# Attention of two layers with each pair of heads stacked in two halves of the partitions

## What is computed

```python
# layer 2, causal, written as an online softmax over key blocks of 128;
# layer 0 is the same without the mask and with biases on q, k, v
scores = scale * jnp.einsum('bhtd,bhsd->bhts', Q, kb)
scores = jnp.where(future[None, None], -jnp.inf, scores)
m_new = jnp.maximum(m, jnp.max(scores, axis=-1, keepdims=True))
p = jnp.exp(scores - m_new)
l = corr * l + jnp.sum(p, axis=-1, keepdims=True)
acc = corr * acc + jnp.einsum('bhts,bhsd->bhtd', p, vb)
return acc / jnp.maximum(l, 1e-12)
```

## Time and profile before

| | |
|---|---|
| median of three runs | 1496.15 us (1493.22 to 1500.85) |
| the profiled execution | 1497.72 us, span 1496.0 us |
| granted TensorE clock, mean | 0.846 |
| busy: PE, DVE, ACT, POOL | 1135.4, 952.6, 614.8, 486.2 us |
| of the chain that ended last: PE, DVE, DMA | 46%, 23%, 7% |

### The profile page before, as it was taken

The page is one execution under the profiler, slowest core; times in us unless marked ns, Lnnn a source line. Parts: engine busy times, 40 slices in busy tenths (PEclk is TensorE's granted clock), DMA queues, the critical chain, the costliest instruction groups (busy, mean ns, idle before and its releaser), DMA issues.

```text
span 1496.0 us, 32177 instructions
## 1 busy us (share of the span) xinstructions
PE 1135.4 (76%) x9171; PEld 822.8 (55%) x9171; DVE 952.6 (64%) x3478; ACT 614.8 (41%) x1352; POOL 486.2 (32%) x695
## 2 busy tenths in 40 slices
PE   2799899889199994776728998999976899337950
PEld 1355555554188883664516776777654566225730
DVE  3688888886423324996836776777557687761237
ACT  1266556656044441335403554555554232113410
POOL 6112433434535453233441111111024111352553
PEclk9599889989599996997657999999977797558985
DMA  4655445531367767211025443444010000133523
GB/s 118 72 59 62 70 67 76 69 59 40 115 196 201 207 198 228 74 43 32 18 31 70 53 53 48 52 55 47 17 29 28 22 25 11 44 110 92 167 78 91
DMA packets 152567, 117.02 MB, mean 78 GB/s; under 512 B 16001, under 2 KB 140674, under 8 KB 152322
## 3 DMA queue, kind: packets, MB, share of 16 engines
q1 hardware_dynamic: 145282, 101.18, 34.2%
q0 software_dynamic: 7168, 14.37, 2.9%
HBM read 47.26 MB, written 23.41 MB: 47 GB/s over the span
## 4 chain that ended last, share of the span: by engine, by line
PE 46%; DVE 23%; issue 10%; DMA 7%; POOL 6%; SPq 3%; ACT 3%; DVEq 1%; POOLq 0%; ACTq 0%
PE po L1485 7%; PE po L431 6%; DVE xg L334 4%; PE pt L1479 4%; DVE mx L601 4%; PE pm L1479 3%; SPq L367 3%; PE pt L391 2%; PE pt L394 2%; PE pm L412 2%; DMA xs<-xg 2%; POOL rstd L327 2%; PE pm L417 2%; PE pm L418 2%; PE p L522 2%
## 5 line engine op out<-in xcount | busy, mean ns | idle before, releaser
L601 DVE TENSOR_REDUCE mx<-pm 128x2 f32<-128x512 f32 (+1 forms) x512 | 306.3, 619 | 163.2 <-PE pm L418 97.8
L553 ACT ACTIVATE ex<-pt 128x512 f32<-128x512 f32 (+1 forms) x512 | 271.1, 544 | 207.9 <-PE pt L391 99.3
L324 POOL TENSOR_SCALAR ve<-mv 128x2 f32<-128x2 f32 x96 | 25.5, 266 | 560.6 <-DVE mv L318 560.6
L1562 POOL DMA_INDIRECT result<-ye,to_row x128 | 122.9, 960 | 151.3 <-issue 107.2
L431 PE MATMUL po<-ex,va 128*32 128x256 f32 (+1 forms) x2048 | 157.7, 381 | 5.2 <-ACT ob L562 5.2
L412 PE MATMUL pm<-ks,qs 96*128 96x256 bf16 x512 | 110.7, 303 | 11.5 <-DVE mx L601 10.9
L308 ACT COPY xt<-p 128x256 f32<-128x256 f32 x112 | 41.8, 373 | 175.1 <-PE p L304 175.1
L1485 PE MATMUL po<-he,we 128*128 128x256 f32 (+1 forms) x448 | 112.9, 395 | 0.6 <-DVE yt L1523 0.4
L334 DVE TENSOR_SCALAR xg<-res,mv,rstd 128x128 f32<-128x128 f32 (+1 forms) x192 | 90.1, 536 | 32.6 <-POOL rstd L327 32.6
L391 PE MATMUL pt<-qs,ks 99*128 99x256 bf16 x512 | 105.7, 292 | 6.4 <-DMA qs<-mt 3.1
L303 PE MATMUL p<-ident,xs 128*128 128x128 f32 x112 | 40.4, 361 | 85.2 <-DMA xs<-xg 81.9
(11 more groups left out here) (281 smaller groups left out, 2788.5 us busy)
## 6 DMA issues: line engine op xcount, KB each, us to landing
we<-in_pack SPq DMA_DIRECT2D x40, 514.5 KB
xs<-xg SPq DMA_DIRECT2D x112, 128.0 KB, 2.2
qs<-parts SPq DMA_DIRECT2D x192, 64.0 KB
ks<-parts SPq DMA_DIRECT2D x192, 64.0 KB
we<-in_pack SPq DMA_DIRECT2D x16, 512.0 KB
xe<-sorted SPq DMA_DIRECT2D x56, 132.0 KB, 2.2
yr<-result SPq DMA_DIRECT2D x48, 128.0 KB, 2.2
xr<-xg SPq DMA_DIRECT2D x32, 128.0 KB, 4.8
```

The source lines that it names most:

```text
L553: nc.scalar.activation(ex[j % 2][:, 2 * u:2 * u + 2, lo:S], pt[:, u, :].rearrange("p (b k) -> p b k", k=S)[:, :, lo:S], ACT.Exp).then_inc( ...
L601: nc.vector.tensor_reduce(mx[q.slot % 2][:, qt, 4 * b + 2 * u:4 * b + 2 * u + 2], pm[:, u, :].rearrange("p (b k) -> p b k", k=S)[:, :, 0:h ...
L1562: pool.indirect_dma_start(out=rows, out_offset=bass.IndirectOffsetOnAxis(ap=to_row[q.slot][0:m, i:i + 1], axis=0), in_=ye[q.slot][0:m, i, ...
```

## The change

A pair of heads shares a slot in `qs` and `ks`: the even head in partitions 0 to 63 (`HALF`), the odd one in 64 to 127. Each has 48 rows of parts and three for the maximum in its half. The tensors are half as wide (`HP` = 8 slots). `scores_t` and `scores_m` become one function, `scores`, that issues a product for the maxima from one half and one for the exponents from the other in turn, after all its waits; in u = 0 the maxima take the even heads and the exponents the odd ones, in u = 1 the other way round. The mask is added by two products a `u` and side, over two heads at once, 128 and 64 columns a head, each from the 64 rows of a half (`half_id`, `hide_k`, `hide_q`). q and k are projected so that even and odd heads land in different halves (`by_half`), the biases are brought into that order once at the start, the maxima are transposed in two pieces, and each stack DMA is now two, one for each half of `parts`. The memsets of the stacks on POOL are gone; DVE fills rows 32 to 63 of each half of `ks` with ones before the data. POOL builds the masks with twelve affine selects in place of two.

```diff
-        hide_k = sb("hide_k", [P, P], BF16)
-        hide_q = sb("hide_q", [P, P], BF16)
+        half_id = sb("half_id", [P, 2, P], BF16)
+        hide_k = sb("hide_k", [P, 2, P], BF16)
+        hide_q = sb("hide_q", [P, 2, P], BF16)
...
-        STACK, MAX_AT = 48, 96
-        ks = [sb(f"ks{i}", [MAX_AT + 3, HEADS, S], BF16) for i in range(SLOTS)]
+        STACK, HALF, HP = 48, P // 2, HEADS // 2
+        ks = [sb(f"ks{i}", [P, HP, S], BF16) for i in range(SLOTS)]
...
-            qs = [sb(f"qs{i}", [MAX_AT + 3, HEADS, S], BF16, mem) for i in range(SLOTS)]
+            qs = [sb(f"qs{i}", [P, HP, S], BF16, mem) for i in range(SLOTS)]
...
-            mx = [sb(f"mx{i}", [P, 2, HEADS], F32, mem) for i in range(2)]
-            mr = [sb(f"mr{i}", [P, 2, HEADS], F32, mem) for i in range(2)]
-            mp = [sb(f"mp{i}", [P, 2, 3, HEADS], BF16, mem) for i in range(2)]
-            mt = [sb(f"mt{i}", [96, P], BF16, mem) for i in range(2)]
+            mx = [sb(f"mx{i}", [P, 2, 2, HP], F32, mem) for i in range(2)]
+            mr = [sb(f"mr{i}", [P, 2, 2, HP], F32, mem) for i in range(2)]
+            mp = [sb(f"mp{i}", [P, 2, 2, 3, HP], BF16, mem) for i in range(2)]
+            mt = [sb(f"mt{i}", [STACK, S], BF16, mem) for i in range(2)]
...
                     sp.wait_ge(mt_sb, a + q.n + 1)
-                    for t in range(2):
-                        sp.dma_start(qs[q.slot][MAX_AT:MAX_AT + 3, :, t * P:t * P + P],
-                                     mt[q.slot % 2][STACK * t:STACK * t + STACK, :]).then_inc(mrows[q.slot], 16)
+                    for of_pair in range(2):
+                        r = HALF * of_pair + STACK
+                        sp.dma_start(qs[q.slot][r:r + 3, :, :],
+                                     mt[q.slot % 2][3 * HP * of_pair:3 * HP * (of_pair + 1), :]).then_inc(mrows[q.slot], 16)
                 if (q := at(1)):
                     wait_apart(sp, parts_pool, 2 * (a + q.n + 1), passed)
+                    if a == 0:
+                        sp.wait_ge(consts_v, CONSTS_V)
+
                     wait_apart(sp, ts_ps, 16 * (a + q.back(3)), passed)
-                    sp.wait_ge(stack_zero, SLOTS * (2 if a == 0 else 3))
-
                     for r, of in enumerate(PAIRS):
                         for i, stack in enumerate((qs, ks)):
-                            sp.dma_start(stack[q.slot][r * DH:r * DH + DH, :, :].rearrange("r h k -> r (h k)"),
-                                         parts[q.slot % 2][:, of[i], i, :]).then_inc(stacked[q.slot], 16)
+                            for of_pair in range(2):
+                                rows_of = slice(HALF * of_pair + r * DH, HALF * of_pair + r * DH + DH)
+                                sp.dma_start(stack[q.slot][rows_of, :, :].rearrange("r h k -> r (h k)"),
+                                             parts[q.slot % 2][HALF * of_pair:HALF * of_pair + HALF, of[i], i, :]
+                                             ).then_inc(stacked[q.slot], 16)
...
+        def by_half(dst, left, right):
+
+            for of_pair in range(2):
+                last = nc.tensor.matmul(dst[HALF * of_pair:HALF * of_pair + HALF], left[:, of_pair::2], right,
+                                        start=True, stop=True)
+            return last
...
-            def scores_t(q, j, u):
...
-            def scores_m(q, j, u):
...
+            def half(stack, q, g, k, at_head):
+
+                return stack[q.slot][HALF * g:HALF * g + k, at_head, :]
+
+            def scores(qt, jt, qm, jm, u):
+
+                gm, gt = u, 1 - u
+                mine, theirs = pm[:, u, :], pt[:, u, :]
+                bm, qtile = jm // 2, jm % 2
+                bt, ktile = jt // 2, jt % 2
+                if qt:
+                    pe.wait_ge(stacked[qt.slot], SPLITS * (a // SLOTS + qt.turn + 1))
+                    pe.wait_ge(mrows[qt.slot], 32 * (a // SLOTS + qt.turn + 1))
+                    wait(pe, e_sb, 16 * (a + qt.n) + 2 * jt + u - 1)
+                if qm:
+                    if jm == 0:
+                        pe.wait_ge(stacked[qm.slot], SPLITS * (a // SLOTS + qm.turn + 1))
+                    wait(pe, ms_max, 16 * (a + qm.n) + 2 * jm + u - 1)
+                if causal:
+                    at_q, at_k = qtile * P, ktile * P
+                    rows_m, rows_t = slice(HALF * gm, HALF * gm + HALF), slice(HALF * gt, HALF * gt + HALF)
+                    for first in (True, False):
+                        lo = 0 if first else HALF
+                        if qm:
+                            dst = mine.rearrange("p (e k) -> p e k", k=S)[:, :, at_q + lo:at_q + P]
+                            pe.matmul(dst, half_id[rows_m, lo // HALF, :],
+                                      hide_q[rows_m, lo // HALF:lo // HALF + 1, lo:P].to_broadcast([HALF, 2, P - lo]),
+                                      start=first, stop=False)
+                        if qt:
+                            dst = theirs.rearrange("p (e k) -> p e k", k=S)[:, :, at_k:at_k + P - lo]
+                            pe.matmul(dst, half_id[rows_t, 1 - lo // HALF, :],
+                                      hide_k[rows_t, 1 - lo // HALF:2 - lo // HALF, 0:P - lo].to_broadcast([HALF, 2, P - lo]),
+                                      start=first, stop=False)
+                for e in range(2):
+                    if qm:
+                        keys = half(ks, qm, gm, STACK, 2 * bm + e)
+                        queries = half(qs, qm, gm, STACK, 2 * bm + e)[:, qtile * P:qtile * P + P]
+                        k0, k1 = (qtile * P, qtile * P + P) if causal else (0, S)
+                        last_m = pe.matmul(mine[:, e * S + k0:e * S + k1], queries, keys[:, k0:k1],
+                                           start=not causal, stop=e == 1 or not causal)
+                    if qt:
+                        keys = half(ks, qt, gt, STACK + 3, 2 * bt + e)[:, ktile * P:ktile * P + P]
+                        queries = half(qs, qt, gt, STACK + 3, 2 * bt + e)
+                        k0, k1 = (ktile * P, ktile * P + P) if causal else (0, S)
+                        last_t = pe.matmul(theirs[:, e * S + k0:e * S + k1], keys, queries[:, k0:k1],
+                                           start=not causal, stop=e == 1 or not causal)
+                if causal:
+                    for e in range(2):
+                        if qm and qtile == 1:
+                            keys = half(ks, qm, gm, STACK, 2 * bm + e)
+                            queries = half(qs, qm, gm, STACK, 2 * bm + e)
+                            last_m = pe.matmul(mine[:, e * S:e * S + P], queries[:, P:S], keys[:, 0:P],
+                                               start=True, stop=True)
+                        if qt and ktile == 0:
+                            keys = half(ks, qt, gt, STACK + 3, 2 * bt + e)
+                            queries = half(qs, qt, gt, STACK + 3, 2 * bt + e)
+                            last_t = pe.matmul(theirs[:, e * S + P:e * S + S], keys[:, 0:P], queries[:, P:S],
+                                               start=True, stop=True)
+                if qm:
+                    last_m.then_inc(ms_ps, 1)
+                if qt:
+                    last_t.then_inc(ts_ps, 1)
...
-                        pe.matmul(p1[:, 0:S], mat(f"q{layer}"), xq, start=True, stop=True)
+                        by_half(p1[:, 0:S], mat(f"q{layer}"), xq)
                     else:
-                        pe.matmul(p1[:, S:2 * S], mat(f"k{layer}"), xq, start=True, stop=True).then_inc(qk_ps, 1)
+                        by_half(p1[:, S:2 * S], mat(f"k{layer}"), xq).then_inc(qk_ps, 1)
...
-                    pe.transpose(p0[0:96, S:2 * S].bitcast(BF16)[:, 0:P],
-                                 mp[q.slot % 2][:, :, :, :].rearrange("p t c h -> p (t c h)"),
-                                 ident16[:, :]).then_inc(mt_ps, 1)
+                    for t in range(2):
+                        last = pe.transpose(p0[0:STACK, S:2 * S].bitcast(BF16)[:, t * P:t * P + P],
+                                            mp[q.slot % 2][:, t, :, :, :].rearrange("p g c h -> p (g c h)"),
+                                            ident16[:, :])
+                    last.then_inc(mt_ps, 1)
...
-                        if (q := at(3) if j >= T0 else at(4)):
-                            scores_t(q, (j - T0) % 8, u)
-                        if (q := at(2) if j >= M0 else at(3)):
-                            scores_m(q, (j - M0) % 8, u)
+                        scores(at(3) if j >= T0 else at(4), (j - T0) % 8, at(2) if j >= M0 else at(3), (j - M0) % 8, u)
...
-                    nc.scalar.activation(ex[j % 2][:, 2 * u:2 * u + 2, lo:S],
+                    nc.scalar.activation(ex[j % 2][:, :, :].rearrange("p (e g) k -> p g e k", g=2)[:, 1 - u, :, lo:S],
...
-                    nc.vector.tensor_reduce(mx[q.slot % 2][:, qt, 4 * b + 2 * u:4 * b + 2 * u + 2],
+                    nc.vector.tensor_reduce(mx[q.slot % 2][:, qt, u, 2 * b:2 * b + 2],
...
```

(14 more changed lines are left out.)

87 lines of the change are left out of this document (31 added, 56 removed).

## The result

The changed kernel takes **1592.3 us** (median of 4 runs, 1583.7 to 1602.8) against 1498.5 of the kernel before in the same session: a ratio of **1.064** (95% interval 1.059 to 1.068), 6% slower. The forecast was 1514 (1448 to 1538): the side was right, the size far off, and the time lies outside the range. The profiled run is the slowest of the four, 1602.8 us with a span of 1601.1.

What follows compares the result with a forecast made beforehand. It took a loop through SP's DMA queue, not PE, to bound layer 2's steps. Layer 0 +13.5, layer 2 +5.5, start -1 gave +18 us on 1497.7, 1515.7; with that run 1.6 above the median, 1514 us, range 1448 to 1538.

Steps and rivals of the forecast that it cites:

- The sum (10.7 + 16.6 + 9.2) / 2: Layer 2, kernel before: x, L and R make a loop over two steps, 18.2 us per step.
- x: Step start until SP starts the next stack DMAs; layer 2 from 10.7 to 9.7 us, layer 0 from 11.3 to 11.2.
- L: Start of SP's stack DMAs until the next `mt` has landed; layer 2 from 16.6 to 19.8 us, layer 0 21.3.
- R: Landing of `mt` until the next step's start; layer 2 from 9.2 to 7.9 us, layer 0 from 9.9 to 8.8.
- The price of the queue: SP's queue, both layers: 0.66 us from start to start per 32 KB stack DMA, 24 taking 15.9 us against 8.0.
- The fill of layer 0's pipeline: First sequences of layer 0: more stack DMAs precede the first `mt`, so step 4 starts at 87.4, +12 us.
- Rival (a): SP's issue price follows size, 0.54 us or below, so PE's saving counts: -40 us, about 1456; chance 22%.
- the forecast sign "in nearly every step of both stages": Attention of layers 0 and 2: if the forecast is right, PE waits for `qs<-mt` in nearly every step.
- The tails: Steps after each layer's last stack, where PE's saving counts: -3 us in layer 0, -4 in layer 2.
- The row halves: Score products in the array's two row halves overlap fully; net PE saving 2.3 us a step in layer 2, 1.7 in layer 0.
- Rival (c): Row halves of the score products do not overlap: +66 us beside the forecast, about 1562; chance 8%.
- rival (b): Queue binds but PE gains more, no shape-change price; steps sit on SP's 18.4 and 19.9 us: 1500; chance 17%.

Runs made afterwards that it cites:

- e1: Kernel before, each of the 12 stack DMAs of a sequence cut in two (24); 1549.9 us, ratio 1.034.
- e2: Changed kernel without the second half's stack DMAs (12 of 32 KB a sequence, zeros in their rows); 1489.8 us, ratio 0.995.
- e7: Changed kernel with the two `xr` DMAs issued ahead of the stack DMAs; 1575.6 us, ratio 1.054.
- e10: Kernel before, with the first exponent product repeated 8 times at j = 3 and j = 4 in layer 0 to fill PE's gaps; 1490.4 us, ratio 0.999.
- e12: e2 plus repeated products on all 128 rows before the groups of j = 2, 3, 4 in layer 0; 1472.8 us, ratio 0.986.
- e13: e9 plus products on all 128 rows before the groups of j = 2, 3, 4 in layer 0; 1545.2 us, ratio 1.031.
- e9: Changed kernel with `xr` ahead of the stacks and the rows of maxima issued before the last 4 of 24 stack DMAs; 1541.9 us, ratio 1.033.
- e11: Kernel before, rows of maxima moved from 96 to 48 so products take 48 and 51 rows, leaving out zeros; 2094.1 us, ratio 1.403.
- e6: e2 with each exponent product on the same half as the max product beside it, so neighbours can't run at once; 1816.3 us, ratio 1.216.
- e3: Changed kernel with the parts written to DRAM once and read back into the stacks by 12 DMAs; 1548.7 us, ratio 1.033.

## Why the prediction was wrong

**What bound the kernel before: misread.** I took one wait of 1.06 us for a sign that SP's queue and not PE ended the steps of layer 2. Over the nine steps of the earlier trace rows PE waited for `mt` only three times, 2.5 us in all, and SP was never late with it: it stood idle until ACT had copied the rows. The sum (10.7 + 16.6 + 9.2) / 2 could not tell, since x, L and R together are two steps by construction, whatever binds. The queue became a bound only with the change; e1 and e2 show that.

**The price of the queue: right.** 0.655 us per DMA of 32 KB, 24 in a row. What the prediction has from a table of the Trainium skill (DMA: Bandwidth & Descriptors), that the saved issue time is usually small beside the DMA, stands in a sentence of its section Issuing engines are not separate DMA queues; here 24 issues filled 15.8 us of a step of 20.8. The fill of layer 0's pipeline came out too: step 4 at 86.8 (forecast 87.4); step 5 of layer 2, where stacking starts 7.9 us behind the second transpose and not 12.4 (forecast 4.5 sooner), 88.3 us behind that transpose (77.9 before; forecast +10 in all). Rival (a) was rightly put aside.

**L: a little too small.** 931.72 to 952.30 is 20.6, forecast 19.8: gaps around `xs` of 0.6 us, and `mt` landed 3.5 us after its first issue, not 3.0.

**x and R: the step that failed.** I took PE's saving off both (9.7 and 7.9 in layer 2). They measured 10.7 (940.40 to 951.11) and 9.45 (952.30 to 961.75). x: here the stacks start 0.24 us behind POOL's last part, in both kernels (the queue itself was late in the steps from 897.09 and 1003.98, where x is 13.1 and 12.4). PE's projections, with which that chain begins, stand at the same place of the step (q at 2.3 and 2.25 us, k at 3.3 and 3.2), and behind them it runs through DVE, ACT and POOL, so PE's saving had no part in x. First the kernel before, in its step from 851.87 (stacks at 862.57), then the changed one:

```profile
861.17 1.16 POOL L718 TENSOR_TENSOR parts<-rem,parts 128x512 bf16<-128x512 f32 x1 [0.73 <-ACT parts L580]
```

```profile
949.72 1.15 POOL L746 TENSOR_TENSOR parts<-rem,parts 128x512 bf16<-128x512 f32 x1 [0.73 <-ACT parts L614]
```

R: the wait of 3.8 us that the longer L brings drops the clock, and half of R then runs at 1.2 GHz. Two steps are (10.7 + 20.6 + 9.45), so 20.4 each, against a measured mean of 20.8 and a forecast of 18.7. The sum used durations at full clock on both sides of a wait that it lengthened itself.

**Layer 0: the wrong path, and two things left out.** Its step was summed by way of `mt` (L = 21.3), and PE waited for `mt` in two of seven steps, 1.6 us in all; the forecast sign "in nearly every step of both stages" held in layer 2 alone (six of nine, two of which the view puts down to "issue" though they end 3.3 us behind the issue of `mt`). `xr` stands behind the stacks in the same queue, and I gave it 1.5 us of issue but no one who waits for it: 24 us of waits in 8 places, worth 1.0 point (e7). And PE's own clock: the kernel before has on average some 4 us at half clock in a step, the changed one some 13. e2 shows it without the queue: with 12 DMAs layer 0 still takes 21.7 us at 0.83. The shorter products lengthen PE's pause before VectorE's maxima, from 1.1 to 1.5 us, and what comes behind it runs at half clock for longer. Steps are 23.3 against a forecast of 20.65. That the pause brings the clock down is shown on the kernel before (e10); on the changed products the fill brought it back only in part (e12, e13), so there it is the likely cause and not a shown one.

**The tails** were to give back 7 us and cost 21.5. They have no stacks for new sequences, but their clock is 0.79 and 0.83, and PE still waits for what the queue had held up. With 12 DMAs (e2) layer 2's tail takes 68.3 us at a clock of 1.00 (71.0 in the kernel before), but layer 0's still 85.4 at 0.84: the queue was the cause in the one, not in most of the other.

**Where the 87 us are** by which the profiled run missed its sum (1602.8 against 1515.7): up to the last stacking step layer 0 lost 43.6 and not 16.5, layer 2 32.4 and not 9.5, which is 50 of them; the tails are 28; 9 are in code that the change does not touch.

**The row halves: right.** They start 0.00 to 0.01 us apart and save 2.06 us of PE at full clock (forecast 2.3). Overlap alone was to give 3.7, so some 1.6 us went elsewhere, 0.14 for each of the 12 changes of shape if it is all theirs: an estimate, since no run takes it apart. Rival (c) fell. Of rival (b), SP's own 18.4 us was the floor I named; it was 19.4 (931.72 to 951.11) in a step in which the queue was full, and in the steps between such SP stood idle for 2.4 to 4.7 us until POOL had the next parts.

By parts: e1 gives the count alone 52 us; the order of SP's queue is worth 46 (e9), though not all of it beside e1, since part is the same waiting; with both count and order out of the way (e2) nothing is left of the loss and 0.5% of a gain.

## What to carry to other kernels

Before a change makes TensorE's work shorter, ask where it will then wait, and what clock it comes back with: time saved before a wait for another engine can be lost behind it. Splitting a DMA cost nearly its full issue price again (0.59 to 0.655 us for each half, 0.66 for the whole), and everything behind it in that queue, not only the data split, arrives later; name each of them and who waits. Rows of zeros in a product can be worth a good deal of time: here the clock stayed at half without them. And a sum of stretches that close a loop is always the loop's length; to show what binds it, look at who stands idle until whom.

## What the runs showed of the hardware

- Products of 48 and 51 rows, one at a time and without a pause, left TensorE at 1.2 GHz for whole stages (e11: 135 us at 0.50 with PE 100% busy; e6: 240 us), where 96 and 99 rows in the same program (half of them zeros) ran at 0.91 to 0.98. Two such products in the two halves at once held 1.00 (e2, layer 2; the changed kernel from 1062.8 to 1096.9). Whether the number of rows counts or the unused half is open.
- The clock column can read 1.00 for hundreds of microseconds where the trace has no clock record (e11, before 605.4 us: 1.00 beside durations of half clock). A group with a known duration, here the eight of L431 at 0.64 or 1.08 us, tells it.
- SP's issue price from SBUF to SBUF was 0.655 us for 32 KB from 64 partitions into 8, and 0.59 for 32 KB into 4 (e1). From DRAM it was 0.32 to 0.39 us for 32 KB in 8 rows and 0.70 to 0.75 for 96 KB in 24 (e3).
